# Cross-attention on one core: the four keys behind the last whole chunk, worked off for all heads at once

## The reference

```python
Q = (input_Q @ W_Q).reshape(b, -1, 16, 64).transpose(0, 2, 1, 3)      # input_Q 1x1024x128
K = (input_K @ W_K).reshape(b, -1, 16, 64).transpose(0, 2, 1, 3)      # input_K = input_V 1x6404x128
V = (input_V @ W_V).reshape(b, -1, 16, 64).transpose(0, 2, 1, 3)
attn = softmax(einsum('bhqd,bhkd->bhqk', Q, K) / 8, axis=-1)
context = einsum('bhqk,bhkd->bhqd', attn, V).transpose(0, 2, 1, 3).reshape(b, -1, 1024)
out = context @ W_O + input_Q
mu, var = mean(out, -1), var(out, -1)
return (out - mu) / sqrt(var + 1e-05)
```

## Time and profile before

| | |
|---|---|
| median of three runs | 1628.64 us |
| profiled execution, its own time | 1629.81 us |
| its span in the trace | 1627.9 us |
| PE busy | 1612.7 us (99%) |
| DVE busy | 1210.3 us (74%) |
| ACT busy | 955.5 us (59%) |
| POOL busy | 58.8 us (4%) |
| chain that ended last | 98% PE; scores 43%, products 43%, works 11% |

### The profile page before, as it was taken

How to read it: one execution, slowest core, us unless ns; L and a number is a source line. 1 busy time by engine, 2 the same in 40 slices (tenths; PEclk the granted TensorE clock), 3 DMA queues, 4 the chain that set the end, 5 groups by cost and what they waited for, 6 DMA issues and landing times.

```text
span 1627.9 us, 39517 instructions
## 1 busy us (share of the span) xinstructions
PE 1612.7 (99%) x17422; PEld 643.8 (40%) x17422; DVE 1210.3 (74%) x1214; ACT 955.5 (59%) x1064; POOL 58.8 (4%) x38
## 2 busy tenths in 40 slices
PE   9999999999999999999999999999999999999997
PEld 3443344333443334433344333443344433444334
DVE  5778787787877778777787777778777787777876
ACT  5556565655556656565655656555665565655652
POOL 0000000000000000000000000000000000000100
PEclk9999999999999999999999999999999999999998
DMA  4000000000000000000000000000000000000000
GB/s 159 2 2 8 2 8 2 1 8 2 8 2 2 8 1 9 2 1 9 1 9 2 2 8 2 9 2 2 8 1 9 2 8 2 2 9 2 8 2 14
DMA packets 12366, 13.76 MB, mean 8 GB/s; under 512 B 4512, under 2 KB 8096, under 8 KB 12192
## 3 DMA queue, kind: packets, MB, share of 16 engines
q1 hardware_dynamic: 11760, 10.61, 2.0%
q10 hardware_dynamic: 432, 0.59, 0.1%
HBM read 10.36 MB, written 0.59 MB: 7 GB/s over the span
## 4 chain that ended last, share of the span: by engine, by line
PE 98%; DVE 1%; DMA 0%; ACT 0%; issue 0%; SPq 0%; ACTq 0%
PE o_ps L374 43%; PE s_ps L357 43%; PE w_ps L421 6%; PE w_ps L404 5%; PE s_ps L444 0%; DMA ctx_all<-in_ctxT 0%; PE o_ps L444 0%; PE w_ps L444 0%; ACT probs L538 0%; DVE sums L637 0%; DVE k_all L625 0%; DVE y L731 0%; DVE limits L741 0%; DVE y L714 0%; PE o_ps L421 0%
## 5 line engine op out<-in xcount | busy, mean ns | idle before, releaser
L637 DVE TENSOR_TENSOR sums<-sums,probs 128x1024 f32<-128x1024 f32 (+1 forms) x800 | 997.6, 1247 | 376.4 <-ACT probs L538 372.3
L538 ACT ACTIVATE probs<-s_ps 128x1024 f32<-128x1024 f32 x816 | 834.9, 1023 | 639.5 <-PE s_ps L357 621.4
L357 PE MATMUL s_ps<-q_sb,k_all 64*64 64x512 f32 x6528 | 847.9, 589 | 0.8 <-DVE q_sb L625 0.6
L374 PE MATMUL o_ps<-probs,v_all 64*64 64x512 f32 x6528 | 847.7, 589 | 0.0
L357 PEld LDWEIGHTS s_ps<-q_sb,k_all 64*64 64x64 f32 x6528 | 251.1, 133 | 449.9 <-issue 447.0
L374 PEld LDWEIGHTS o_ps<-probs,v_all 64*64 64x64 f32 x6528 | 246.8, 133 | 390.8 <-issue 385.5
L404 PEld LDWEIGHTS w_ps<-wv_sb,ctx_all 64*64 64x64 f32 x3232 | 97.2, 133 | 57.6 <-issue 51.8
L421 PE MATMUL w_ps<-ctx_all,wk_sb 64*64 64x512 f32 (+1 forms) x832 | 107.1, 585 | 0.5 <-DMA ctx_all<-in_ctxT 0.5
L404 PE MATMUL w_ps<-wv_sb,ctx_all 64*64 64x128 f32 x3232 | 106.9, 269 | 0.4 <-DVE k_all L625 0.4
L625 DVE TENSOR_TENSOR k_all<-k_all,w_ps 128x512 f32<-128x512 f32 (+1 forms) x104 | 69.6, 670 | 6.8 <-ACT k_all L546 6.8
L332 POOL TENSOR_TENSOR o_b<-o_a,o_b 128x512 f32<-128x512 f32 x15 | 31.5, 2097 | 1116.2 <-ACT o_a L568 1116.2
(11 more groups left out here) (59 smaller groups left out, 104.8 us busy)
## 6 DMA issues: line engine op xcount, KB each, us to landing
inv_sum<-inv_dram SPq DMA_DIRECT2D x30, 128.0 KB, 2.8
ctx_all<-in_ctxT SPq DMA_DIRECT2D x12, 256.0 KB, 5.6
quad_rows<-quad_sums SPq DMA_DIRECT2D x60, 4.0 KB, 1.7
xT_sb<-in_xT ACTq DMA_DIRECT2D x2, 256.0 KB, 4.6
x_sb<-in_x SPq DMA_DIRECT2D x1, 512.0 KB, 10.1
wo_sb<-in_wo SPq DMA_DIRECT2D x1, 512.0 KB, 11.1
out<-y SPq DMA_DIRECT2D x4, 128.0 KB, 1.8
wq_sb<-in_wq SPq DMA_DIRECT2D x1, 448.0 KB, 6.9
```

The lines of the kernel that those rows point to most:

```text
L357: last = nc.tensor.matmul(s_ps[part(half), u % 2, head * QH:(head + 1) * QH], k_all[part(head), c * P + half * DH:c * P + (half + 1) * DH] ...
L374: last = nc.tensor.matmul(o_ps[part(head), rows, :], v_all[part(rows), c, part(head)], probs[part(rows), u % RING, head * QH:(head + 1) * QH],
L538: nc.scalar.activation(probs[:, u % RING, :], s_ps[:, u % 2, :], ACT.Exp, scale=SCALE).then_inc(probs_ready, 1)
L637: nc.vector.tensor_tensor(out=sums[0:rows, t % 2, :], in0=sums[0:rows, t % 2, :], in1=probs[0:rows, u % RING, :], op=ALU.add).then_inc(sum ...
```

## The change

The keys are split in 50 whole chunks and 4 keys left. All passes but the last run over 50 chunks (801 units in place of 816); the last pass (t = 15) still has its 51st chunk. In pairs 0 to 6 the tail block of K and V has 256 columns in place of 384.

For the other 15 passes the 4 keys left are computed once for all heads, in six works of the first pass, at chunks 15, 17, 19, 21, 23 and 25, between the works of K and V that stand at the even chunks: K of the 4 keys for all heads ("kl"), V of them ("vl"), W_Q turned over ("wt"), W_Q K^T for all heads ("gl", 64 columns: 16 heads by 4 keys), the scores of all heads and 1024 queries in one work ("sl"), and V W_O ("vw"). ACT takes their exponential at chunk 27 into `p_left`. SP copies the rows of a pass from `p_left` to `left_rows`, DVE adds them to the pass's sums at chunk 40 (`add_left`), and SP loads each pass's inverse sums also into `inv_left`. POOL multiplies `p_left` by it once, and each output tile gets one more matmul, `p_left` by `vw_left`.

In the first stage the first chunk of keys is loaded, computed and copied by itself ("a"), and q of block 0 as full 128-row matmuls without an addition, ACT and DVE each copying a half; the rest of block 0 of K has 384 columns; `scores(0)` goes ahead of the work v. The second half of `xT` is loaded by SP after block 1 of the context. In the last stage the tiles of the projection are finished one after the other, the test of the range stands between the second and the third group of the layer norm, and SP loads the choice before its last two stores.

```diff
-    UNITS = PASSES * CHUNKS
+    FULL_CHUNKS = NK // P
+    UNITS = PASSES * FULL_CHUNKS + 1
+    LEFT_ROWS = 2 * PAIRS * LEFT
+    LEFT_STEP, LEFT_EXP_STEP = 40, 27
+    LEFT_WORK = {15: "kl", 17: "vl", 19: "wt", 21: "gl", 23: "sl", 25: "vw"}
...
-    WARM_UP = 2
+    WARM_UP = 4
...
+    def chunks_of(t):
+        return CHUNKS if t == PASSES - 1 else FULL_CHUNKS
...
-    FIRST = [("k", 0, 0), ("q", 0, 0), ("v", 0, 0)]
+    FIRST = [("a", 0, 0), ("q", 0, 0), ("k", 0, 0), ("v", 0, 0)]
...
+            if b < FULL_BLOCKS:
+                return BK
+            return TAIL_COLS if pair == PAIRS - 1 else LEFT_AT - TAIL_AT
...
             sp.dma_start(wk_sb[:, 0:2 * DH], w_k[:, 0:2 * DH]).then_inc(first_w_loaded["k"], 16)
-            load_ctx(0)
+            sp.dma_start(ctx_all[:, 0:P], ctxT[:, 0:P]).then_inc(chunk_loaded, 16)
+            sp.dma_start(ctx_all[:, P:BK], ctxT[:, P:BK]).then_inc(ctx_loaded[0], 16)
             sp.dma_start(wv_sb[:, 0:2 * DH], w_v[:, 0:2 * DH]).then_inc(first_w_loaded["v"], 16)
-            for b in range(1, BLOCKS):
+            load_ctx(1)
+            sp.dma_start(xT_sb[:, QH:NQ], xT[:, QH:NQ]).then_inc(x_loaded[1], 16)
+            for b in range(2, BLOCKS):
...
+            def load_left(t):
+                pair, h = t // 2, t % 2
+                if t == 0:
+                    sp.wait_ge(left_ready, 1)
+                else:
+                    sp.wait_ge(left_added, t)
+                for head in range(2):
+                    row = h * DH + (2 * pair + head) * LEFT
+                    sp.dma_start(left_rows[:, head * QH:(head + 1) * QH], p_left[row:row + LEFT, :]).then_inc(left_loaded, 16)
...
+                for head in range(2):
+                    row = t % 2 * DH + (t // 2 * 2 + head) * LEFT
+                    sp.dma_start(inv_left[row:row + LEFT, :], inv_dram[t, head * QH:(head + 1) * QH]
+                                 .partition_broadcast(LEFT)).then_inc(inv_left_loaded, 16)
+                if t + 1 < PASSES - 1:
+                    load_left(t + 1)
...
+            def left_work(found):
+                kind = found[0]
+
+                pe.wait_ge(work_ready, COUNT[found] - 1)
+                pe.wait_ge(rest_w_loaded, 48)
+                if kind in ("kl", "vl"):
+                    pe.wait_ge(ctx_loaded[FULL_BLOCKS], 16)
+                    w_sb = wk_sb if kind == "kl" else wv_sb
+                    for pair in range(PAIRS):
+                        for rows in range(2):
+                            for head in range(2):
+                                at = pair * P + head * DH
+                                last = nc.tensor.matmul(w_ps[part(head), rows, pair * LEFT:(pair + 1) * LEFT],
+                                                        w_sb[part(rows), at:at + DH], ctx_all[part(rows), LEFT_AT:NK],
+                                                        start=True, stop=True)
...
+            for found in FIRST[:3]:
                 work(found)
-            for u in range(AHEAD):
-                scores(u)
+            scores(0)
+            work(FIRST[3])
+            scores(1)
...
+                    if pair == 0 and left:
+                        h, at = t // (QT // 2), t % (QT // 2) * P
+                        nc.tensor.matmul(y_ps[t], p_left[:, at:at + P], vw_left[:, h, :], start=False, stop=False)
...
-            for t in (4, 5):
-                project_output(t, range(PAIRS - 1))
+            project_output(4, range(PAIRS - 1))
+            pe.wait_ge(last_norm_done, 1)
+            project_output(4, [PAIRS - 1]).then_inc(y_done, 1)
+            project_output(5, range(PAIRS)).then_inc(y_done, 1)
...
+            project_output(6, range(PAIRS)).then_inc(y_done, 1)
+
+            pe.wait_ge(y_taken, 2)
...
+            project_output(7, range(PAIRS)).then_inc(y_done, 1)
...
+            def add_left(t):
+
+                dve.wait_ge(left_loaded, 32 * (t + 1))
+                dve.wait_ge(sums_done, FULL_CHUNKS * t + LEFT_STEP + AHEAD + 1)
+                nc.vector.tensor_tensor(out=sums[0:LEFT, t % 2, :], in0=sums[0:LEFT, t % 2, :], in1=left_rows[:, :],
+                                        op=ALU.add).then_inc(left_added, 1)
...
                 if u + AHEAD < UNITS:
                     add_sums(u + AHEAD)
+                if t < PASSES - 1 and c == LEFT_STEP:
+                    add_left(t)
                 found = work_at(t, c)
```

More of the change, by code:

```diff
@@ L301, in general, with store @@
                 g_loops(sp, load_weights, g_nothing, load_blocks)
-            def store(turn):
-                for n in range(QT // 2):
+            def store(turn, groups):
+                for n in groups:
                     sp.wait_ge(ln_done, QT * turn + 2 * n + 2)
@@ L381, in work @@
                 banks = banks_of(found)
+                if kind == "a":
+                    pe.wait_ge(first_w_loaded["k"], 16)
+                    pe.wait_ge(chunk_loaded, 16)
+                    nc.tensor.matmul(banks[0][:, 0:P], wk_sb[:, 0:P], ctx_all[:, 0:P],
+                                     start=True, stop=True).then_inc(work_done, 1)
+                    return
+                if found in WHOLE:
+                    pe.wait_ge(first_w_loaded["q"], 16)
+                    pe.wait_ge(x_loaded[0], 16)
+                    for n in range(2):
+                        last = nc.tensor.matmul(banks[n][:, 0:QH // 2], wq_sb[:, 0:P],
+                                                xT_sb[:, n * (QH // 2):(n + 1) * (QH // 2)], start=True, stop=True)
+                    last.then_inc(work_done, 1)
+                    return
+                if found == FIRST[3]:
+                    pe.wait_ge(work_half, COUNT["q", 0, 0])
+                    pe.wait_ge(work_ready, COUNT["q", 0, 0])
                 if found not in FIRST:
@@ L426, in _ @@
             for _ in range(WARM_UP):
-                nc.tensor.matmul(s_ps[0:DH, 0, 0:QH], ones[:, :], o_a[:, :], start=True, stop=True)
-            for found in FIRST:
+                nc.tensor.matmul(s_ps[0:DH, 0, 0:QH // 2], ones[:, :], o_a[:, 0:QH // 2], start=True, stop=True)
+            for found in FIRST[:3]:
                 work(found)
-            for u in range(AHEAD):
-                scores(u)
+            scores(0)
+            work(FIRST[3])
+            scores(1)
             for u in range(UNITS):
@@ L435, in _ @@
                     scores(u + AHEAD)
-                found = work_at(u // CHUNKS, u % CHUNKS)
-                if found is not None:
+                found = work_at(*place(u))
+                if found is not None and found[0] in LEFT_WORK.values():
+                    left_work(found)
+                elif found is not None:
                     work(found)
@@ L555, in _ @@
+            take_half(FIRST[3])
+            exps(1)
             for u in range(UNITS):
-                t, c = u // CHUNKS, u % CHUNKS
+                t, c = place(u)
                 if u + AHEAD < UNITS:
@@ L559, in _ @@
                 found = work_at(t, c)
-                if found is not None:
+                if found is not None and found[0] in LEFT_WORK.values():
+                    take_left(found)
+                elif found is not None:
                     take_half(found)
-                if c == CHUNKS - 1:
+                if t == 0 and c == LEFT_EXP_STEP:
+                    act.wait_ge(work_ready, COUNT["sl", 0, 0])
+                    nc.scalar.activation(p_left[:, :], p_left[:, :], ACT.Exp, scale=SCALE).then_inc(left_ready, 1)
+                if c == chunks_of(t) - 1:
                     act.wait_ge(pv_done, u + 1)
@@ L628, in add_sums @@
             def add_sums(u):
-                t, c = u // CHUNKS, u % CHUNKS
-                rows = LAST_KEYS if c == CHUNKS - 1 else P
+                t, c = place(u)
+                rows = LAST_KEYS if c == FULL_CHUNKS else P
                 dve.wait_ge(probs_ready, u + 1)
@@ L672, in _ @@
             for u in range(UNITS):
-                t, c = u // CHUNKS, u % CHUNKS
-                if c == CHUNKS - 1 and t < PASSES - 1:
+                t, c = place(u)
+                if c == chunks_of(t) - 1 and t < PASSES - 1:
                     dve.wait_ge(pv_done, u + 1)
@@ L704, in _, with layer_norm @@
                                     op=ALU.mult).then_inc(last_norm_done, 1)
-            def layer_norm(turn):
+            def layer_norm(turn, groups):
                 STEPS = 5
-                for n in range(QT // 2):
+                for n in groups:
                     before = STEPS * (QT // 2 * turn + n)
```

227 lines of the change are left out of this document (184 added, 43 removed).

## The result

The changed kernel takes 1613.16 us (median of five runs, 1612.76 to 1613.79) against 1628.89 (1628.42 to 1629.18): a ratio of 0.9904, interval 0.9892 to 0.9917. 15.7 us were won, 19.6 were forecast; the time lies inside the range. The span of the profiled execution fell from 1627.9 to 1611.8, by 16.1 us. All times here are of executions at a mean granted clock of 0.997 or more; one execution of an experiment (half first), 1646.59 us at 0.97, is left out.

A forecast was written before the change was run, and what follows sets the result against it. PE was taken to bound the kernel nearly throughout. The terms -25.8 - 3.0 + 5.9 + 4.0 + 3.4 - 0.7 - 3.4 sum to -19.6 us, giving a forecast of 1609.0 us, range 1603.5 to 1614.

The forecast's parts named there:

- rival 2: Small works on PE go by instructions, 27 ns each, 1.74 us a work: +3.5 us, 1612.5 us; chance 19%.
- Units and tail blocks: Passes on PE: 15 units of 1.72 us go, -25.8 us; 14 tail works shrink by 0.22, -3.0 us.
- The six works on PE: First pass: four small works at 0.87, "sl" 0.86, "vw" 1.6; +5.9 us, ends 4.6 and 9.4.
- The wait behind a neighbouring work: Chunks 15 to 25: each of six odd works waits 0.67 us for `w_ps`; +4.0 us, ends 0 and 8.
- The rows added on DVE: Chunk 40: `add_left` delays DVE's half, so PE waits before chunk 42's work; +3.4 us, ends 0 and 5.
- The first stage: Start: `scores(0)` 1.7 us earlier, of which 0.7 arrives at v of block 1; -0.7 us, ends -1.7 and +0.3.
- The last stage: End: choice written before the last two norm groups, last store ends the run; -3.4 us, ends -5 and -1.
- rival 4: End: the long branch stays last, on DVE or SP; +2.1 us, 1611.1 us; chance 10%.
- Weight loads that nothing covers (1): Five works with many matmuls: 316 weight loads run one after the other; +36.9 us, 1646 us; chance 3%.
- No wait at chunk 42 (3): Chunk 42: DVE's backlog from the added rows is absorbed; -3.4 us, 1605.6 us; chance 17%.

The follow-up runs named there:

- half first: The changed kernel with the added rows' addition still at chunk 40, but behind DVE's half of that chunk's work: 1607.06 us, ratio 0.9865.

## Why the prediction was right, and which terms were off

1613.16 lies 4.2 above the forecast of 1609.0 and near the upper end of the range, and 0.7 from rival 2's 1612.5. That nearness is chance: rival 2's mechanism did not act, and the difference came from the terms below.

*Units and tail blocks*, -25.8 and -3.0: right. The kernel with this alone is 28.9 us faster.

*The six works on PE*: 5.9 forecast, 6.5 measured. "sl" and "vw" were within 0.05 of the forecast; the four small ones take 0.95 to 0.98 and not 0.87, with 4 columns or 64. An instruction is 0.015 us, a step over four quadrants 0.058, far from v's 0.109 and from the lower end of 0.027. The forecast's 0.87 was the middle between two bounds and not a reading, so it is in part luck that it came near. The Trainium skill's rule ("TensorEngine Tiling (Array Packing)", Instruction Overhead), by which one column costs as much as 60, had given an estimated 0.82; the trace agrees with its kind, as 4 and 64 columns cost the same, and its size was 0.13 low.

*The wait behind a neighbouring work*: 4.0 forecast, 4.2 measured, at the six odd works and nowhere between, and gone when the works have no neighbour. Right, from one such wait in the trace of before.

*The rows added on DVE*: 3.4 forecast, 6.0 measured. This is the term that was mis-sized, and it makes most of the 3.5 us by which the forecast of the span missed. The mechanism was right (moving it behind one instruction of DVE returns all of it); what was missing is 0.12 of the 0.18 that the addition's wait for DVE's own last sum costs, and about 0.06 of PE's starting up after a wait: 0.18 in each of 15 passes, 2.7 us, against the 2.6 that were missing. For the odd passes the trace has it piece by piece: 4.57 us from the end of the scores to PE's next work in pass 1 where 4.46 was forecast, and PE there after 4.31 (4.30).

*The first stage*: -0.7 forecast, -0.9 between the two traces, 0.5 to 0.8 at an equal moment of the clock's rise. The steps (1.7 ahead at the scores, nearly half of it given back in DVE's chain) came as written. The times of whole runs can't confirm it.

*The last stage*: -3.4 forecast, -3.2 measured. The choice was written 15.6 after the work d (forecast 16.0), the last norm ended 20.2 after it (20.6), and the store followed; DVE's branch then added some 0.6, which is rival 4's mechanism, on DVE, at a third of its size.

*The rivals.* Weight loads that nothing covers (1): out, 64 loads and matmuls take 0.95 together. 27 ns each (2): out, they take 15. The Trainium skill's floor of about 25 ns ("TensorE: Matmul & The Clock Gate", Wait — 56ns, not 53.3ns?) is not shared by the quadrants: in one quadrant 58 ns pass from start to start, over all four 15. No wait at chunk 42 (3): out, the wait was longer.

## What to carry to other kernels

Where engines work through one hand-written order, the place of an added step matters more than its length: 15 additions of 1.2 us on an engine 75% busy cost 6 us ahead of an instruction that PE waits for, and nothing behind it. When steps share one buffer, put them two units apart; one wait of that kind in the trace of before was enough here to price the six that the change added. What every engine must read or branch on at the end should be decided before the last work, so that the branch runs beside it.

## What the runs showed of the hardware

Four-column fp32 matmuls in four quadrants, each with its weight load, pass at 15 ns an instruction, and 64 columns take hardly more (0.98 against 0.95 for 64 instructions). PE counted as busy all the time in such a stretch, but once, after 0.68 us of waiting and 1.9 us of it, the granted clock fell to 1.2 GHz for 3.4 us and cost 1.7 us. After a second such stretch (0.67 of waiting, 1.9) it stayed at 2.4 GHz, and after 0.95 us of it as well.

A DVE instruction that waits for its own engine's last one starts 0.10 us after that one's end, and otherwise 0.08 before it.

A branch over the general program takes PE 3.3 to 3.9 us in eleven traces and 1.2 in one (the small matmuls twice). DVE's program ended 0.6 us after its branch began in the kernel before and in the one with the units removed, and 2.8 to 3.4 after it in the ten traces of kernels built on the changed one. The kernel with the last stage of before is one of these ten (2.8), so the order of norm and test does not explain it; why is open.
